# Copies moved between two engines, one load moved to another queue, and one product moved earlier, in a one-core adaLN, attention and routed-FFN kernel

## What is computed

```python
# 1. low-rank layer whose weights are scaled by a condition vector per sequence
w_down = down_project * (cond @ down_gamma) + (cond @ down_beta)     # 256 x 64
w_up   = up_project   * (cond @ up_gamma)   + (cond @ up_beta)       # 64 x 256
h = relu(x @ w_down) @ w_up + x
# 2. attention: 8 heads, 5 sigmoids a head; the likeness of two tokens is a sum of
#    running products of agreements; causal softmax; values h @ Wv, out @ Wo
x = x + attention(h, Wp, bp, Wv) @ Wo
# 3. a weight matrix made from the condition: U = cond @ W_dec + b_dec (257 x 30 a sequence)
z = x @ (U[:-1] @ V) + U[-1] @ V
# 4. routed layer, top 1 of 8 experts, residuals
x = x + z + expert[argmax(z @ gate_w.T)](z)
```

## Time and profile before

| | |
|---|---|
| median of 3 runs | 150.49 us (150.21 to 151.03) |
| the profiled execution, its own time | 150.60 us |
| its span, first to last instruction | 148.9 us |
| PE busy | 138.3 us (93%) |
| PE weight load busy | 87.3 us |
| DVE busy | 99.5 us (67%) |
| ACT busy | 56.3 us (38%) |
| POOL busy | 49.0 us (33%) |
| mean granted PE clock | 0.989 |
| moved by DMA | 12.62 MB |

### The profile page before, as it was taken

How to read it: one execution, slowest core, us unless ns; L and a number is a source line. 1 busy time by engine, 2 the same in 40 slices (tenths; PEclk the granted TensorE clock), 3 DMA queues, 4 the chain that set the end, 5 groups by cost and what they waited for, 6 DMA issues and landing times.

```text
span 148.9 us, 4940 instructions
## 1 busy us (share of the span) xinstructions
PE 138.3 (93%) x2190; PEld 87.3 (59%) x2190; DVE 99.5 (67%) x186; ACT 56.3 (38%) x67; POOL 49.0 (33%) x71
## 2 busy tenths in 40 slices
PE   5999679999988999999899999999999998999992
PEld 5646346655535577665565766556557674667651
DVE  0473737883998746689957567699376967984431
ACT  3013370544543132558414344473235466310010
POOL 7200056006062632453075336600665651200000
PEclk9999999999998699999999999999999999999999
DMA  4999999910022000000011100011011010111212
GB/s 108 324 362 424 409 358 350 317 39 0 2 33 31 6 4 4 0 4 0 0 40 42 35 2 4 4 35 40 0 35 40 4 35 7 35 38 37 70 39 72
DMA packets 7381, 12.62 MB, mean 85 GB/s; under 512 B 1552, under 2 KB 5808, under 8 KB 7232
## 3 DMA queue, kind: packets, MB, share of 16 engines
q1 hardware_dynamic: 7120, 11.86, 22.8%
q0 software_dynamic: 96, 0.05, 0.8%
q10 hardware_dynamic: 144, 0.39, 0.7%
HBM read 10.09 MB, written 2.22 MB: 83 GB/s over the span
## 4 chain that ended last, share of the span: by engine, by line
PE 69%; DVE 19%; issue 5%; POOL 3%; ACT 3%; DVEq 0%; POOLq 0%; ACTq 0%
PE work L656 37%; PE c_ps L656 16%; PE s_ps L656 12%; DVE tiles L596 3%; DVE rden L481 2%; DVE feat L646 2%; DVE tiles L599 2%; ACT prob L428 2%; PE work L787 2%; POOL zo L411 2%; PE work L847 2%; DVE phi_t L546 1%; DVE h_t L529 1%; PE work L839 1%; DVE tiles L592 1%
## 5 line engine op out<-in xcount | busy, mean ns | idle before, releaser
L428 ACT ACTIVATE prob<-s_ps 128x1536 f32<-128x1536 f32 (+1 forms) x24 | 38.3, 1594 | 41.5 <-PE s_ps L656 41.5
L392 POOL TENSOR_SCALAR_AFFINE_SELECT prob<-prob 128x1024 f32<-128x1024 f32 x16 | 18.0, 1127 | 70.1 <-ACT prob L428 70.1
L481 DVE RECIPROCAL rden<-c_ps 128x256 f32<-128x256 f32 x16 | 28.1, 1754 | 6.7 <-PE c_ps L656 6.7
L656 PE MATMUL s_ps<-phi_t 32*128 32x256 f32 (+1 forms) x384 | 24.1, 365 | 1.1 <-DVE phi_t L546 0.6
L656 PEld LDWEIGHTS s_ps<-phi_t 32*128 32x128 f32 x384 | 17.4, 184 | 11.7 <-issue 8.5
L656 PE MATMUL c_ps<-prob,v_sb 128*32 128x256 f32 (+1 forms) x384 | 22.8, 356 | 0.0
L404 POOL TENSOR_TENSOR short<-prob 128x512 f32<-128x512 f32 x15 | 20.2, 1346 | 1.3
L656 PE MATMUL work<-ctx_t,mix_sb 128*32 128x256 f32 x256 | 17.0, 381 | 0.5 <-ACT zo_t L463 0.2
L656 PE MATMUL work<-zo_t,gexp 128*32 128x256 f32 x256 | 16.9, 379 | 0.0
L656 PEld LDWEIGHTS c_ps<-prob,v_sb 128*32 128x32 f32 x384 | 11.0, 111 | 9.0 <-issue 3.2
L656 PE MATMUL work<-w_vl,h_t 128*32 128x296 f32 x208 | 15.1, 415 | 0.4 <-DVE h_t L529 0.4
(11 more groups left out here) (109 smaller groups left out, 154.2 us busy)
## 6 DMA issues: line engine op xcount, KB each, us to landing
wdec<-in_W_dec SPq DMA_DIRECT2D x1, 3855.0 KB, 18.3
x_t<-in_x_tr SPq DMA_DIRECT2D x4, 512.0 KB, 9.0
ex_t<-in_expert_tr SPq DMA_DIRECT2D x1, 2048.0 KB, 25.3
out_x<-x_t SPq DMA_DIRECT2D x16, 128.0 KB, 1.7
mix_sb<-in_mix SPq DMA_DIRECT2D x1, 904.0 KB, 19.9
lift_sb<-in_lift ACTq DMA_DIRECT2D x1, 384.0 KB, 4.0
w_vl<-in_vl SPq DMA_DIRECT2D x1, 296.0 KB, 5.2
first_sb<-in_first SPq DMA_DIRECT2D x1, 144.0 KB, 3.6
```

The source lines that it names most:

```text
L392: nc.gpsimd.affine_select(out=tri, in_=tri, compare_op=ALU.is_ge, fill=0.0, base=0, pattern=[[0, HG], [0, 2], [1, P]], channel_multiplier= ...
L428: nc.scalar.activation(prob[:, p % 2, :, 0:width(p)], s_ps[:, :, 0:width(p)], ACT.Exp).then_inc(exped, 1)
L481: link(nc.vector.reciprocal(rden[:], c_ps[m % 2][:, CW:2 * CW]))
L656: return nc.tensor.matmul(o, w, r, start=start, stop=stop, skip_group_check=True)
```

## The change

`U` 0 to 2 and `lift` 2 and 3 are copied out of PSUM by ACT instead of DVE; `U` 3 stays on DVE. `scaler` changes: for sequence 1 ACT scales both head groups, for sequences 2 and 3 DVE scales group 0 and ACT group 1 (it was the other way round). `lift_sb` is loaded by SP, second in its queue. `down` of sequence 1 stands in front of `phi` of sequence 0, FIRST, and has bank 0; `phi` SECOND of sequence 0 stands in the prologue in front of `scores` 1. An opening pair's `add(p)` stands in front of `context(p)`, behind the steps of `after_scores`, instead of behind the steps of `after_context` of pair p-1. SP waits for the copies of `U` 1 and 2 as well. With the order of steps, work banks 0 and 1 change places for most later steps.

```diff
 def scaler(s):
-    return "scalar" if s[2] == 0 and s[3] != SECOND else "vector"
+    if s[3] == ALL_T:
+        return "scalar" if s[2] == 1 or s[1] == 1 else "vector"
+    return "scalar" if s[2] == 0 and s[3] == FIRST else "vector"
...
             ("VL", 0, 0), ("VL", 0, 1), *features(0, FIRST), ("feat", 0, FIRST), ("VL", 0, 2), ("VL", 0, 3), ("bias", 0, SECOND),
-            ("phi", 0, 0, FIRST), ("phi", 0, 1, FIRST), ("tanh", 0, SECOND), ("scores", 0), ("feat", 0, SECOND),
-            ("down", 1)]
+            ("down", 1), ("phi", 0, 0, FIRST), ("phi", 0, 1, FIRST), ("tanh", 0, SECOND), ("scores", 0),
+            ("feat", 0, SECOND), ("phi", 0, 0, SECOND), ("phi", 0, 1, SECOND)]
 EARLY_BANK = {("gdn", (0,)): 0, ("gup", 0): 1, ("down", 0): 2, ("gdn", (1, 2, 3)): 3, ("up", 0, 0): 4, ("up", 0, 1): 5,
-              ("gup", 1): 0, ("VL", 0, 0): 1, ("VL", 0, 1): 2, ("VL", 0, 2): 4, ("VL", 0, 3): 5,
+              ("gup", 1): 0, ("VL", 0, 0): 1, ("VL", 0, 1): 2, ("VL", 0, 2): 4, ("VL", 0, 3): 5, ("down", 1): 0,
...
     if b == 0:
-        gaps[0] = [("phi", b, 0, SECOND), ("phi", b, 1, SECOND)] + gaps[0]
...
-        ORDER += _a + [("context", _p)]
+        ORDER += _a
+        if opening(_p):
+            ORDER += [("add", _p)]
+        ORDER += [("context", _p)]
         ORDER += _c
-        if _p + 1 < ALL and long(_p + 1):
+        if _p + 1 < ALL and long(_p + 1) and not opening(_p + 1):
             ORDER += [("add", _p + 1)]
...
             sp.dma_start(first_sb[:], first).then_inc(ld_first, 16)
+            sp.dma_start(lift_sb[:], lift).then_inc(ld_lift, 16)
...
                 if s == ("U", 3):
+                    done(sp, ("U", 2))
+                    done(sp, ("U", 1))
                     done(sp, s)
...
         def _(act):
-            act.dma_start(lift_sb[:], lift).then_inc(ld_lift, 16)
...
+                elif s[0] == "U" and s[1] < 3:
+                    m = s[1]
+                    full(act, s)
+                    nc.scalar.copy(u_row[:, U_PIECE * m:U_PIECE * (m + 1)], bank(s)[:, 0:U_PIECE]
+                                   ).then_inc(empty(s), 1)
+                elif s[0] == "lift":
+                    full(act, s)
+                    nc.scalar.copy(w_up[:, s[1], :], bank(s)[:, 0:D]).then_inc(empty(s), 1)
...
-                elif kind == "lift":
-                    full(dve, s)
-                    nc.vector.tensor_copy(w_up[:, s[1], :], bank(s)[:, 0:D]).then_inc(empty(s), 1)
...
-                    full(dve, s)
-                    nc.vector.tensor_copy(u_row[:, U_PIECE * m:U_PIECE * (m + 1)], bank(s)[:, 0:U_PIECE]
-                                          ).then_inc(empty(s), 1)
+                        nc.vector.tensor_copy(u_row[:, U_PIECE * m:U_PIECE * (m + 1)], bank(s)[:, 0:U_PIECE]
+                                              ).then_inc(empty(s), 1)
```

## The result

Median 148.22 us (4 executions, 147.9 to 148.48) against 150.41 (150.21 to 151.03): ratio 0.985, interval 0.981 to 0.989. The change is 2.2 us faster; 2.5 were forecast (150.49 to 148.0). The profiled execution took 148.48 us with a span of 146.8.

A forecast was written before the change was run, and what follows sets the result against it. PE, busy 93% of the span, was taken as the bound, so gains come where it waits or its clock is low. 1.0 + 0.7 + 1.4 - 0.55 = 2.55 us off 150.60 gave 148.0 for the median; range 146.9 to 149.8.

The forecast's parts named there:

- Part 2: Head: lift_sb's load second on SP, ahead of x, taken as 0; bounds a 0.1 us gain and 0.7 loss.
- Part 1: Head: `down` 1 put behind the values and phi SECOND ahead of scores 1, starting `up` 1 earlier; gain 1.0 us.
- Part 5: Later sequences: opening sums moved and phi's engines swapped; net loss 0.55 us, bounds -1.2 and +0.3.
- Part 3: Around 36 to 45 us: copies and phi moved from DVE to ACT; 0.7 us gain beyond the head's.
- Part 4: 47.00 to 50.75 us: PE's low stretch before it shrinks and the clock stays up; gain 1.4 us, bounds 0 and 1.7.
- A: Head: the clock falls there instead, after about 20 us, costing 1.4 us; 149.4 us; chance 20%.
- B: Near 44 to 47 us: the clock falls all the same, so its 1.4 us gain is lost; 149.4; chance 13%.
- C: Held sums or the U round trip hide DVE's relief and half the clock's gain; 149.9 us; chance 11%.
- E: Head: x loads late behind lift_sb's load on SP; 148.7 us, inside the forecast's range, no separate chance.
- D: Clock falls in the head and for a second 3.75 us stretch, and the old fall stays; 152.5 us; chance 4%.

The follow-up runs named there:

- head alone: The kernel before with only the new prologue (`down` of sequence 1 ahead of phi FIRST, phi SECOND ahead of scores 1): median 147.79 us, ratio 0.982.
- the load alone moved back: The changed kernel with only lift_sb's load back on ACT: 147.00 and 146.91 us, 149.71 and 149.80 at clock 0.988; ratio 0.977 from the first two.
- old sums: The changed kernel with opening sums at their old place, 147.57 us; with lift_sb's load also back on ACT, 147.24 us.
- the filler: The kernel before with three unread 128x256 products added on PE ahead of ubT of sequence 0: 149.27 us against 150.46, ratio 0.992.
- the copies alone: The kernel before with only U 0 to 2, lift 2 and 3 and phi of sequence 1 group 1 on ACT: 148.70 us, ratio 0.989.

## Why the prediction was right, point by point

- **Time, sign and range**: 148.0 forecast, 148.22 measured, inside 146.9 to 149.8. The profiled execution's sum of 2.55 came out at 2.1, through errors of both signs: part 2 cost 0.80 that was put at nothing, and part 1 brought 0.3 more than forecast. That the total came so close is in part luck, and so is part 5's.
- **Part 1**: 1.0 forecast, 1.3 measured, in the changed kernel and in the head alone. The term that was too small is the 0.3 by which phi was to start late. `down` 1 starts with the last values still in flight: 16.16 against a nominal end of 16.37 (13.17 + 3.20), and phi came only 0.05 later against the start. The rest, 0.65 + 0.38, was as worked out: `up` 1 follows scores 1 and lasts 1.14.
- **Part 2**: taken at 0, with a loss of 0.7 as bound. It cost 0.80 in the profiled execution, where PE waited 1.62 us for x, and nothing to 1.4 us of waiting in others. The step that failed is the slack of 0.75 against 0.45 of delay: the landing of x was taken as the shortest of its kind, moved by the delay of its issue, but behind lift_sb on the same queue it took 5.8 us here instead of 4.9 (and 4.4 to 5.6 in the four other traces with this order). The first load did land sooner (the copy that needs it starts at 3.01 instead of 4.44), and that gained nothing, since the warm-up covers it: PE's first step began at 5.16 or 5.17 in three of the five traces with this order, as before. The 4.84 of the profiled execution came with a shorter warm-up (3.42 us, 3.78 before). What the load costs in the median is known only roughly: 1.2 by the two executions at full clock with the load alone moved back, 0.3 by the pair of kernels with old sums (147.57 and 147.24). An estimate from more executions: behind `down` 0 the traces of the changed kernel, and of the three that differ from it in a load or in phi alone, take 139.0 to 139.1 us, and with the sums moved back and phi on ACT 138.5. Taken off the spans at full clock, that leaves starts of `down` 0 with a median of 7.4 in 16 executions with lift_sb ahead of x on SP, and 6.9 in 13 with it on ACT: some 0.5. The Trainium skill, "DMA: Bandwidth & Descriptors", section "Queues, rings and completion order", says that each DMA engine takes turns between the queues it has work for; the first load's earlier landing, once the second one stood behind it on its own queue, agrees.
- **Part 3**: 0.7 forecast, 0.78 measured. The hold of DVE's sums by POOL was right in place and size: the closing sum took 1.77 us, ending 0.56 behind POOL's where 0.54 was said, and the opening one 1.94. The attribution was only half right. phi's 0.66 is there, but in the new order it costs nothing on DVE either; I had worked out parts 3 and 5 separately and not seen that the sum's new place, behind phi, hides phi in the hold.
- **Part 4**: 1.4 forecast, 1.36 measured in the pair of traces, and its cause shown by the filler. What I had not put into the forecast is that it is a matter of frequency: 4 of 27 executions of the kernel before hold the clock, and 8 of 10 of the changed one.
- **Part 5**: 0.55 forecast, 0.53 measured. Sequence 2 came out at +0.20 (forecast -0.05) and the end at +0.33 (0.35); in sequence 1 the expected 0.25 did not come, as POOL's sum ended just when DVE's closing sum began:

```profile
72.78 2.13 POOL L411 TENSOR_TENSOR short<-prob 128x512 f32<-128x512 f32 x1
...
74.91 0.68 DVE L606 TENSOR_TENSOR tiles<-tiles,prob 128x512 f32<-128x512 f32 x1
```

  There, with phi as in the change, the new place is the better one by 0.34, which the forecast did not see either. So 0.53 is luck: in sequence 2 the held sum cost 0.53 (9.26 against 8.73 with the old place) where 0.25 was said, in sequence 1 nothing where 0.25 was said, and the two errors cancelled. The gain from phi's new engine was right: 0.33 (9.06 to 8.73), 0.3 forecast.
- **Rivals**: A (the clock falls in the head) appeared in no trace. B, the fall near 45 all the same, is by their mean clock what 2 of 10 executions did, at 149.7 and 150.1 where 149.4 was said; neither has a trace, so where their clock fell isn't shown. C did not come: the copies alone gained 0.78 and held the clock. E came in the head of the profiled execution, inside the range as said. D's second stretch was seen in the trace of the head alone, behind 45 us and not in the head.

## What to carry to other kernels

A wait on TensorE is worth more than its length when the granted clock falls behind it: here filling 1.3 us of waiting with useless products gained 1.2 us in the median. Before a sum on DVE is put ahead of or behind a PSUM copy, look at what POOL runs then; the copy runs beside it and the sum of two SBUF tiles does not, so the copy goes first. And a load that is put into a queue ahead of another has to be weighed by when the second is wanted, in more than one execution.

## What the runs showed of the hardware that I had not expected

- The hold between DVE and POOL works both ways and passes on: a sum that started first stretched POOL's mask from 1.10 to 1.88 us, and 2.5 us later POOL's sum stretched DVE's from 0.68 to 1.21.
- The first product of 512 columns took 1.02 to 1.92 us in different executions of nearly the same head, with the granted clock at 1.00 each time, which by itself moves the start of `down` 0 by up to 0.9 where x is there.
- One traced execution had 7 us at half clock behind a wait of 1.3 us, where the other three of that kernel, by their mean clocks of 0.998 to 1.0, had next to none.
